# The output stage of a hyperbolic attention layer: scaling, limiting and the residual add regrouped on VectorE

## The reference, cut to what matters

```python
def _project(x):
    sp = jnp.clip(x[..., 1:], -8.0, 8.0)
    x0 = jnp.sqrt(1.0 + jnp.sum(sp ** 2, axis=-1, keepdims=True) + EPS)
    return jnp.concatenate([x0, sp], axis=-1)
...
return _project(_exp_map(mu, out @ Wo.T))
...
x = x + _L1_attn_ref(_layernorm(x, axis=-1), L1_attn_Wq, ...)
x = x + _L1_ffn_ref(_layernorm(x, axis=-1), ...)
```

## Time and profile before

| | before |
|---|---|
| three runs, median (lowest to highest) | 2600.14 us (2599.54 to 2600.92) |
| the profiled execution, its own time | 2600.85 us |
| its span in the trace | 2599.0 us |
| mean granted TensorE clock over the span | 0.938 |
| TensorE busy, share of the span | 86% |
| ScalarE busy | 57% |
| VectorE busy | 49% |
| GpSimd busy | 15% |

### The profile page before, as it was taken

How to read it: one execution, slowest core, us unless ns; L and a number is a source line. 1 busy time by engine, 2 the same in 40 slices (tenths; PEclk the granted TensorE clock), 3 DMA queues, 4 the chain that set the end, 5 groups by cost and what they waited for, 6 DMA issues and landing times. The chain is left out here.

```text
span 2599.0 us, 41169 instructions
## 1 busy us (share of the span) xinstructions
PE 2240.9 (86%) x12824; PEld 1055.9 (41%) x12825; DVE 1263.2 (49%) x2727; ACT 1492.3 (57%) x2466; POOL 383.1 (15%) x628
## 2 busy tenths in 40 slices
PE   4996799933979999999999999999057999999993
PEld 3783455522642222222222222225034666666662
DVE  5566522246884444444444444421465444444444
ACT  2213433224748999999999999997553222222220
POOL 0030266641000000000000000000001222222220
PEclk9998899976988999999999999999578999999996
DMA  5001122241100000000000000003263444344445
GB/s 180 1 1 65 45 77 79 75 176 69 34 9 1 1 1 1 1 1 1 1 1 1 1 1 1 1 1 115 80 183 99 119 119 119 119 120 120 120 116 211
DMA packets 105458, 160.19 MB, mean 62 GB/s; under 512 B 9465, under 2 KB 81905, under 8 KB 105329
## 3 DMA queue, kind: packets, MB, share of 16 engines
q1 hardware_dynamic: 90544, 117.05, 14.8%
q0 software_dynamic: 13632, 37.24, 4.4%
q10 hardware_dynamic: 1152, 4.19, 0.4%
HBM read 118.86 MB, written 35.39 MB: 59 GB/s over the span
## 5 line engine op out<-in xcount | busy, mean ns | idle before, releaser
L1681 ACT ACTIVATE at_pexp<-at_psS 128x1024 f32<-128x1024 f32 x1024 | 968.0, 1023 | 59.8 <-PE at_psS L1581 56.8
L1695 DVE TENSOR_REDUCE at_mx<-at_psM 128x1 f32<-128x512 f32 x474 | 327.4, 691 | 478.3 <-PE at_psM L1608 478.3
L1595 PE MATMUL at_psO<-at_pexp,at_vst 128*32 128x512 f32 x4096 | 546.4, 605 | 0.1
L1581 PE MATMUL at_psS<-l1c_QT,l1c_KT 64*128 64x512 f16 x2048 | 403.9, 387 | 12.2 <-ACT at_pexp L1681 6.1
L1581 PEld LDWEIGHTS at_psS<-l1c_QT,l1c_KT 64*128 64x128 f16 x2048 | 100.4, 92 | 617.0 <-ACT at_pexp L1681 556.0
L2008 PE MATMUL ex_psH<-wide_wgu,ex_xT 128*128 x852 | 339.9, 549 | 0.1
L2052 ACT ACTIVATE ex_sg<-ex_bias 128x228 f32<-128x228 f32 x213 | 83.7, 393 | 288.1 <-DVE ex_bias L2078 255.1
L2078 DVE TENSOR_TENSOR ex_bias<-ex_psH,ex_bias 128x456 f32<-128x456 f32 x213 | 134.7, 633 | 198.4 <-PE ex_psH L2008 192.9
L2008 PEld LDWEIGHTS ex_psH<-wide_wgu,ex_xT 128*128 128x128 f32 x852 | 157.2, 191 | 138.5 <-issue 138.4
L1005 POOL DMA_INDIRECT expert_rows<-ex_y,ex_odx x142 | 140.4, 989 | 397.4 <-issue 286.0
L2031 PE MATMUL ex_psY<-wide_w2b,ex_hT 114*128 (+1 forms) x852 | 196.0, 379 | 0.7 <-DVE ex_y L2097 0.7
(11 more groups left out here) (337 smaller groups left out, 2631.5 us busy)
## 6 DMA issues: line engine op xcount, KB each, us to landing
ex_bias<-in_L_ffn_bg SPq DMA_DIRECT2D x71, 342.0 KB
ex_bias<-in_L_ffn_b SPq DMA_DIRECT2D x71, 342.0 KB
normed<-rt_area SPq DMA_DIRECT2D x16, 512.0 KB, 2.6
lm_y<-expert_rows SPq DMA_DIRECT2D x16, 512.0 KB
cb_y<-expert_rows SPq DMA_DIRECT2D x16, 512.0 KB, 7.6
w_raw<-in_L_ffn_w SPq DMA_DIRECT2D x24, 256.0 KB
wide_wgu<-in_L_ffn_Wg SPq DMA_DIRECT2D x8, 684.0 KB
wide_wgu<-in_L_ffn_W SPq DMA_DIRECT2D x8, 684.0 KB
```

The source lines that it names most:

```text
L1581: mm = pe.matmul(psS[:, n, hh * BANK:(hh + 1) * BANK], keys(k.KT, p)[r, kt * P:(kt + 1) * P], keys(k.QT, p)[r, c * BANK:(c + 1) * BANK], s ...
L1595: mm = pe.matmul(psO[g * VW:(g + 1) * VW, y, :], vst[:, p % 2, hh, kt, :], pexp[:, (p * ST + step) % 3 * 2 + n, hh * BANK:(hh + 1) * BANK] ...
L1681: act.activation(pexp[:, u % 6, :], psS[:, u % 2, :], ACT.Exp, scale=D ** -0.5 / (QS * QS)).then_inc(raised, 1)
L1695: dve.tensor_reduce(mx[:, n:n + 1], psM[:, :], AX.X, ALU.max).then_inc(reduced, 1)
```

## The change

Scaling moves from ScalarE to VectorE, where one instruction for each tile multiplies by `g` and applies the lower limit; a second one for each group applies the upper limit. The add of the old stream moves ahead of the making of channel 0: it takes channels 1 to 255 of a group, one group behind the scaling, once ScalarE has squared that group. Channel 0 of the old stream is copied aside into a new array `x0`, and is added when channel 0 is written. The statistics of all 32 tiles follow in one go.

```diff
+        x0 = s.sb("x0", [P, NT])
...
-                dve.sem_inc(asked, 1)
-                for n in range(NG):
-                    part = u[:, n * G:(n + 1) * G, :]
-                    dve.wait_ge(scaled, (n + 1) * G)
-                    dve.tensor_scalar(part, part, -8.0, 8.0, ALU.max, ALU.min).then_inc(clipped, 1)
+                for n in range(NG + 1):
+                    if n < NG:
+                        part = u[:, n * G:(n + 1) * G, :]
+                        for t in range(n * G, (n + 1) * G):
+                            dve.tensor_scalar(u[:, t, :], u[:, t, :], g[:, t:t + 1], -8.0, ALU.mult,
+                                              ALU.max).then_inc(scaled, 1)
+                        dve.wait_ge(scaled, (n + 1) * G)
+                        dve.tensor_scalar(part, part, 8.0, None, ALU.min).then_inc(clipped, 1)
+                    if n:
+                        m = n - 1
+                        part = u[:, m * G:(m + 1) * G, 1:C]
+                        dve.wait_ge(x2_in[m % XR], (m // XR + 1) * 16)
+                        dve.tensor_copy(x0[:, m * G:(m + 1) * G], x2[:, m % XR, :, 0])
+                        dve.wait_ge(squared, NT + (m + 1) * G)
+                        dve.tensor_tensor(part, part, x2[:, m % XR, :, 1:C], ALU.add).then_inc(added, 1)
                 dve.wait_ge(squared, 2 * NT)
                 ser(dve.tensor_scalar(s2[:, :], s2[:, :], 1.0, EPS, ALU.add, ALU.add))
                 dve.sem_inc(asked, 1)
                 dve.wait_ge(done_act, 4)
-                dve.tensor_copy(u[:, :, 0], s2[:, :]).then_inc(led, 1)
+                dve.wait_ge(added, NG)
+                dve.tensor_tensor(u[:, :, 0], s2[:, :], x0[:, :], ALU.add).then_inc(led, 1)
                 dve.wait_ge(led, 1)
-                for n in range(NG):
-                    part = u[:, n * G:(n + 1) * G, :]
-                    dve.wait_ge(x2_in[n % XR], (n // XR + 1) * 16)
-                    dve.tensor_tensor(part, part, x2[:, n % XR, :, :], ALU.add).then_inc(added, 1)
-                    dve.wait_ge(added, n + 1)
-                    for t in range(n * G, (n + 1) * G):
-                        dve.bn_stats(k.st6[:, t, :], u[:, t, :])
+                for t in range(NT):
+                    dve.bn_stats(k.st6[:, t, :], u[:, t, :])
...
-                act.wait_ge(asked, 3)
-                act.wait_ge(u_out, NPR)
-
-                def scale(n):
-                    for t in range(n * G, (n + 1) * G):
-                        act.activation(u[:, t, :], u[:, t, :], ACT.Copy, scale=g[:, t:t + 1]).then_inc(scaled, 1)
-
-                scale(0)
                 for n in range(NG):
-                    if n + 1 < NG:
-                        scale(n + 1)
                     act.wait_ge(clipped, n + 1)
                     for t in range(n * G, (n + 1) * G):
                         act.wait_ge(squared, NT + t)
                         act.activation(junk[:, 1:C], u[:, t, 1:C], ACT.Square,
                                        accum_out=s2[:, t:t + 1]).then_inc(squared, 1)
-                act.wait_ge(asked, 4)
+                act.wait_ge(asked, 3)
                 act.activation(s2[:, :], s2[:, :], ACT.Sqrt).then_inc(done_act, 1)
```

## The result

The changed kernel takes 2585.17 us (median of six runs, 2582.35 to 2585.97), the kernel before 2600.53 us in six runs (2598.66 to 2601.85). The ratio is 0.9939, with a 95% interval of 0.9926 to 0.9952: 0.6% faster, 15.4 us between the medians. Forecast were 2585.5 us and a range of 2583.5 to 2590.2.

What follows compares the result with a forecast made beforehand. Two serial pieces bound the stage: ScalarE's scaling and squares, then VectorE's adds and statistics. Gains of 5.0 and 9.9 us, 0.1 lost between, cut 51.7 to 36.85; 14.9 off the whole gave 2585.5 us, range 2583.5 to 2590.2.

Steps and rivals of the forecast that it cites:

- The bound of the first piece: Scaling and squares, before channel 0: VectorE becomes the bound at 3.02 us a group, in place of ScalarE's 3.61.
- The price of a scaling: VectorE's scaling of a tile: 345 ns, 0.263 us from start to start, 1.16 us a block of four with its wait.
- The block of 1.41 us: Four scalings on VectorE without overlap, by the strict reading: 0.25 us more a block, gain 13.1 us.
- the dearer rows: Scaling priced by L1227 (408 ns, gain 13.1 us) or L2097 (483 ns, gain 10.8); dearer than the likeliest case: 0.16.
- The small terms: On VectorE: copy of old channel 0 0.12 us, add 1.21 with the next 1.13 later, 32 statistics 10.7.
- The cover of the last add: Between squares and statistics: ScalarE's 1.28 us table load covers the add; 1.9 us where it was 1.8; uncovered, 1.2 more.
- The old stream's loads: Loads 4 and 7, issued 10.7 and 8.9 us before wanted, stay hidden; the rival, late and slower, had 0.03.
- The 5.0 us taken for a landing: Median time in which a load lands, set against loads issued 10.7 and 8.9 us before they are wanted.
- the rival of two engines slowing each other: VectorE's adds and scalings beside ScalarE's squares: gain under 5.2 us if 36.85 became 46.5; no change had 0.04.
- Its split of the gain: Stage's 14.9 us: about 5.0 in scaling and squares, 9.9 from adds leaving the last piece, 0.1 lost between.

Runs made afterwards that it cites:

- tile_of_four_on_scalare: Changed kernel with one tile of each group scaled by ScalarE again and both bounds in the group's one limit: 2584.45 us, stage 34.95 us.
- ring_of_1: Changed kernel with one place instead of four groups in the ring for the old stream: 2599.08 us, stage 50.45 us.
- ring_of_2: Changed kernel with a ring of two groups instead of four for the old stream: 2585.12 us, stage 36.65 us.
- root_before_last_add: Changed kernel with the small instruction that readies the sums for the root moved ahead of the last add: 2585.93 us (one run), stage 36.66 us.

## Why the prediction was right

*The bound of the first piece.* "VectorE becomes the bound, at 3.02 in place of 3.61": measured 2.98. Shown by the waits, which turned, and by the two experiments that change VectorE's list: without the adds the bound goes to the squares, and with one scaling less the round falls by the 0.26 us of one scaling. ScalarE's squares have a room of 0.76 us a group (2.98 against 2.22).

*The price of a scaling.* L1257's row was taken, 345 ns and 0.263 from start to start; measured 348 ns, and four in 1.14 us, which is (1.14 - 0.348) / 3 = 0.264. The constant bound is free, as assumed: without it, in tile_of_four_on_scalare, a scaling takes 348 ns too. The block of 1.41 us, in which one scaling ends before the next begins, did not come, nor did the dearer rows.

*The small terms.* The copy of 128x4 takes 0.16 and advances the list by 0.07 (0.12 assumed); the add of four rows of 255 takes 1.22, one run of 1024 took 1.21 to 1.23; the statistics 10.55 (10.7 assumed). These small differences leave the start of the statistics 26.11 us after g (26.15 assumed), so nearly all of the 0.2 us between 36.85 and 36.66 is the statistics.

*The cover of the last add.* From squares to statistics 1.9 us was assumed, 0.1 more than before, and 1.92 measured against 1.79. So the add is not free, as the prediction's word has it, but costs the 0.1 us that its sum has.

*The old stream's loads.* Issued at 1838.66 and hidden with room to spare; ring_of_1 puts a number on what lateness costs. The 5.0 us taken for a landing was the middle between 6.2 and 3.8 and not the price of these loads, which changed nothing here.

*The neighbours.* Adds and scalings beside ScalarE's squares keep their durations (four scalings take 1.14 us in the first group, with no square yet, and 1.14 later), so the rival of two engines slowing each other has nothing in it for VectorE and ScalarE. For VectorE and GpSimd it is real.

*What the prediction did not say.* Its split of the gain, 5.0 from scaling and 9.9 from the adds, is what each piece of the timeline loses, not what each edit is worth. Alone the edits are worth 9.7 and 9.9; the second one made brings 5.1 to 5.4, whichever it is. The sum was right because it was made on the combined lists.

*What was luck.* The stage was forecast at 36.85 and measured at 36.66, which the lists explain. That the time came within 0.3 us of the forecast is in part luck: the runs of the changed kernel alone spread over 3.6 us, the forecast lay between two bases 0.7 apart, and of the 15.7 us by which the span fell 0.6 came from outside the stage.

## What to carry to other kernels

Write out the list of each engine for one round and compare the sums: the gain of moving work is the difference of the larger sums, and two moves that are each free can use the same room. Where a stage ends in a barrier and has two serial pieces held by different engines, work that has no need of the second piece's input (here an add that does not touch channel 0) belongs under the first. Before an idle engine gets work, see what it shares with the one that is the bound; the place for GpSimd here was beside the statistics, and not beside the scaling.

## What the runs showed of the hardware that was not expected

A GpSimd add of 128x1020 and VectorE's scaling, limiting and small add into channel 0 exclude each other for the whole instruction: a scaling of 0.35 us took 2.44, a limit of 0.69 us took 2.85, and two instructions on 32 elements took 1.45 and 1.97 instead of 0.17 and 0.21. Statistics of 128x256 (10.55 us for 32) did not notice it at all.

The landing time of a load of 512 KB went with when it was issued, and a median over both kinds hides it. The last four in the kernel before landed in 3.8 us, and those issued behind an add or in the first piece in 3.5 to 3.7 in the other profiles that give a figure. The first four land in 4.7 to 6.2 us: they are issued together, with the expert weights behind them, and the DMA engines move 411 GB/s from 1790 to 1795 in the kernel before. With a ring of two the two first loads take 4.0, and with one the single first load 3.7. That fits loads which slow each other; no run here tests it by itself.

The moment at which g is ready lies between 1828.04 and 1835.56 us in eleven profiles, although the work in front of it is the same but for the number of early loads. So two kernels whose stages differ by 2 us can't be ranked by one profiled span; the stage's own length, which repeated to 0.01 us where nothing on the path had changed (changed 36.66, ring_of_2 36.65, root_before_last_add 36.66), can.
